# Second attention of a two-layer gated block: layer-norm moments finished in three pieces on two engines, four scalings on VectorE, a tail that is only centred, and context first in the gate matmuls

## The reference, cut to what matters

```python
# third block (q = layernorm(x), k = v = context)
x3 = jnp.concatenate([q, k, v], axis=-1)
ig, fg = x3 @ igate_kernel + igate_bias, x3 @ fgate_kernel + fgate_bias
C = qk * exp(log_D - max_log_D)          # decay from the cumulated forget gate
h = C / (maximum(|sum(C)|, exp(-max_log_D)) + 1e-6) @ v
h_norm = (h - mean) * rsqrt(var + 1e-5) * outnorm_scale
x = x + tanh(g_xattn[1]) * h_norm
# fourth block
xn = layernorm(x)
scale = max(max(|xn|), 1e-6) / 127       # one number for the whole tensor
h = round(xn / scale) @ round(w1 / sw).T ...
```

## Time and profile before

| what | before |
|---|---|
| median of three runs | 1289.48 us (1284.91 to 1289.98) |
| profiled execution | 1283.37 us |
| its span | 1281.6 us |
| TensorE busy | 1178.7 us, 92% |
| VectorE busy | 1089.0 us, 85% |
| ScalarE busy | 1001.3 us, 78% |
| GpSimd busy | 837.2 us, 65% |
| mean granted TensorE clock | 0.984 |

### The profile page before, as it was taken

How to read it: one execution, slowest core, us unless ns; L and a number is a source line. 1 busy time by engine, 2 the same in 40 slices (tenths; PEclk the granted TensorE clock), 3 DMA queues, 4 the chain that set the end, 5 groups by cost and what they waited for, 6 DMA issues and landing times.

```text
span 1281.6 us, 30879 instructions
## 1 busy us (share of the span) xinstructions
PE 1178.7 (92%) x11660; PEld 842.2 (66%) x11660; DVE 1089.0 (85%) x1710; ACT 1001.3 (78%) x1727; POOL 837.2 (65%) x1313
## 2 busy tenths in 40 slices
PE   4699999999999999999998999999899898389898
PEld 3377777777777777777764666666777676144387
DVE  3488989899899899888888899999648889779987
ACT  1288888878878888788776999999555767689896
POOL 3148687776877778777767788876215878877100
PEclk9999999999999999999999999999999989599999
DMA  8677887777878787767622000001555554055099
GB/s 154 116 156 139 172 170 147 161 143 165 163 129 183 147 167 147 134 120 127 112 69 68 1 2 1 1 2 42 162 154 134 126 161 114 0 234 226 1 360 363
DMA packets 127972, 165.71 MB, mean 129 GB/s; under 512 B 47554, under 2 KB 80450, under 8 KB 124354
## 3 DMA queue, kind: packets, MB, share of 16 engines
q1 hardware_dynamic: 127056, 162.95, 53.9%
q10 hardware_dynamic: 768, 0.79, 0.5%
HBM read 78.69 MB, written 33.03 MB: 87 GB/s over the span
## 4 chain that ended last, share of the span: by engine, by line
PE 51%; POOL 18%; DVE 10%; ACT 9%; issue 6%; DMA 3%; SPq 2%; ACTq 0%; DVEq 0%; POOLq 0%
PE psum L617 7%; PE psum L632 6%; PE psum L2284 4%; PE psum L599 4%; PE psum L587 3%; POOL rs L937 3%; PE psum L1090 3%; PE psum L644 3%; ACT f_gelu L2340 3%; PE psum L662 3%; PE psum L1131 2%; POOL norm_rstd L135 2%; PE psum L562 2%; PE psum L1659 2%; POOL a_fac L1986 2%
## 5 line engine op out<-in xcount | busy, mean ns | idle before, releaser
L745 ACT ACTIVATE exp_t<-psum 128x512 f32<-128x512 f32 x512 | 278.4, 599 | 98.6 <-PE psum L617 98.6
L817 DVE TENSOR_REDUCE neg_max<-psum 128x8 f32<-128x1024 f32 x256 | 312.4, 1220 | 32.1 <-PE psum L599 25.1
L937 POOL TENSOR_TENSOR rs<-rs,minus_half 128x16 f32<-128x16 f32 x64 | 187.2, 2925 | 5.0
L617 PEld LDWEIGHTS psum<-q_stack,k_stack 50*128 50x128 f32 x2048 | 133.4, 186 | 74.5 <-ACT exp_t L745 39.5
L617 PE MATMUL psum<-q_stack,k_stack 50*128 50x128 f32 x2048 | 169.7, 285 | 0.5 <-ACT exp_t L745 0.5
L599 PE MATMUL psum<-k_stack,q_stack 48*128 48x256 f32 x1024 | 119.5, 310 | 19.8 <-DVE neg_max L817 16.8
L632 PE MATMUL psum<-exp_t,v_pad 128*32 128x256 f32 x2048 | 137.1, 385 | 0.7 <-DVE x_state L848 0.7
L1090 PE MATMUL psum<-f_w,f_xqt 128*128 128x512 bf16 x512 | 121.4, 379 | 1.9 <-DVE f_hid L1251 1.3
L929 POOL TENSOR_TENSOR sq<-u 128x256 f32<-128x256 f32 x64 | 39.2, 612 | 116.4 <-DVE u L838 116.4
L107 DVE BATCH_NORM_STATS2 norm_stats<-x_state 128x6 f32<-128x256 f32 x256 | 102.0, 412 | 12.0 <-DMA x_state<-in_x 11.4
L734 ACT ACTIVATE q_stack<-psum 128x512 fp32r<-128x512 f32 x128 | 76.0, 594 | 29.5 <-PE psum L587 29.5
(11 more groups left out here) (256 smaller groups left out, 2939.7 us busy)
## 6 DMA issues: line engine op xcount, KB each, us to landing
k_stack<-k_hi SPq DMA_DIRECT2D x252, 128.0 KB, 4.4
k_stack<-k_lo SPq DMA_DIRECT2D x126, 128.0 KB, 4.5
g_scratch<-f_gelu SPq DMA_DIRECT2D x14, 1024.0 KB, 4.2
f_gelu<-g_scratch SPq DMA_DIRECT2D x9, 1024.0 KB, 12.5
ctx_t<-in_ctx_t SPq DMA_DIRECT2D x32, 256.0 KB, 5.2
x_state<-in_x SPq DMA_DIRECT2D x16, 512.0 KB, 6.6
v_in<-in_ctx SPq DMA_DIRECT2D x32, 256.0 KB, 4.2
v_scratch<-v_in SPq DMA_DIRECT2D x32, 256.0 KB, 4.5
```

Source lines behind the costliest of these rows:

```text
L617: r = e.matmul(psum[:, bank + j, o:o + P], self.k_st[rows, b // 2 % self.NK, pair // 2 % 2, pair % 2, i, pair // 4, b % 2, :], self.q_st[r ...
L745: e.activation(self.prob[:, n % 3, j].rearrange("p n w t -> p (n w t)"), psum[:, self.score_bank(n) + j, :], ACT.Exp).then_inc(s["exp"], 1)
L817: e.tensor_reduce(self.negm[:, b % 2, :, :, 2 * u:2 * u + 2].rearrange("p j w n -> p j n w"), psum[:, 0:2, :].rearrange("p j (n w k) -> p ...
L937: e.tensor_tensor(self.rs[:, i], self.rs[:, i], self.expo[:, :], ALU.pow).then_inc(s["pool"], 1)
```

## The change

- `gates`: the two context chunks are issued first, the two from `a_qt` last; for the first twelve groups the wait for `a_qt` stands between them.
- The moments of the first six groups of eight sequences (`SPLIT = 6`) are no longer finished by `finish` at i = 4g+9. `finish_first` (three sums, GpSimd) is issued at i = 4g+9, `finish_middle` (three operations, now ScalarE; the square takes one operation where there were two) and `finish_last` (a sum and the power, GpSimd) at i = 4g+11. The last three groups keep `finish`.
- `next_normed` and `next_max` of a pair come two iterations later and catch up at i = 33 and 34.
- VectorE does `scaled` for the pairs 6, 8, 28 and 30; before it did so for 30 alone.
- The last eight pairs instead of the last two are only centred. Four of them are written in the tile `a_sq`, so that they need not wait for `next_max` to free the ring of four.
- `keep_busy`: four matmuls at each second value of `next_max`.
- ScalarE's `act_normalise` 2 and 3 for the fourth block move from i = 34 to i = 43.

```diff
--- before.py
+++ after.py
@@ -73,7 +73,7 @@
         self.b_gate = self.sb("a1_bgate", [P, 1])
         self.s = self.sems("", ("const_loaded", "gates_loaded", "gates_ready", "made", "steps", "out_written"))
         self.n = [self.sems(f"norm{k}_", ("moments", "rstd")) for k in range(2)] * 2
-        self.finished, self.finishes = None, 0
+        self.finished, self.finishes, self.split_finishes = None, 0, 0
         self.s_x = [self.sem(f"x_in{i}") for i in range(4)]
 
     def sb(self, name, shape, dt=F32):
@@ -108,7 +108,7 @@
 
     def finish(self, w, k, g):
 
-        e, n, done = w.e, self.n[k], self.finishes
+        e, n, steps = w.e, self.n[k], 8 * self.finishes + 7 * self.split_finishes
         first, size = self.GROUPS[k][g]
         self.finishes += 1
         rows, i = slice(first, first + size), first % 16
@@ -122,17 +122,51 @@
...
-        w.wait_ge(self.s["steps"], 8 * done + 8)
+        w.wait_ge(self.s["steps"], steps + 8)
         e.tensor_tensor(self.rstd[:, rows], var, self.expo[:, 0:size], ALU.pow).then_inc(n["rstd"], 1)
+
+    def finish_parts(self, k, g):
+
+        first, size = self.GROUPS[k][g]
+        i = first % 16
+        two = lambda c: (self.stats[:, k % 2, i:i + size, c], self.stats[:, k % 2, i:i + size, c + 3])
+        return first, size, two, [self.work[:, j, 0:size] for j in range(3)], 8 * sum(len(a) for a in self.GROUPS[:k]) + 7 * g
+
+    def finish_first(self, w, k, g):
+
+        first, size, two, (var, total, apart), _ = self.finish_parts(k, g)
+        w.wait_ge(self.n[k]["moments"], self.moments_made(k, first + size))
+        w.wait_ge(*self.finished)
+        w.e.tensor_tensor(apart, *two(1), ALU.subtract).then_inc(self.s["steps"], 1)
+        w.e.tensor_tensor(total, *two(1), ALU.add).then_inc(self.s["steps"], 1)
+        w.e.tensor_tensor(var, *two(2), ALU.add).then_inc(self.s["steps"], 1)
+
+    def finish_middle(self, w, k, g):
+
+        first, size, _, (var, total, apart), steps = self.finish_parts(k, g)
+        w.wait_ge(self.s["steps"], steps + 3)
+        w.e.activation(self.neg_mean[:, first:first + size], total, ACT.Copy, scale=-0.5).then_inc(self.s["steps"], 1)
+        w.e.activation(var, var, ACT.Copy, scale=1.0 / D, bias=1e-5).then_inc(self.s["steps"], 1)
+        w.e.activation(apart, apart, ACT.Square, scale=0.5).then_inc(self.s["steps"], 1)
+
+    def finish_last(self, w, k, g):
+
+        first, size, _, (var, _, apart), steps = self.finish_parts(k, g)
+        self.split_finishes += 1
+        self.finished = (self.n[k]["rstd"], self.groups_made(k, first))
+        w.wait_ge(self.s["steps"], steps + 6)
+        w.e.tensor_tensor(var, var, apart, ALU.add).then_inc(self.s["steps"], 1)
+        w.wait_ge(self.s["steps"], steps + 7)
+        w.e.tensor_tensor(self.rstd[:, first:first + size], var, self.expo[:, 0:size], ALU.pow).then_inc(self.n[k]["rstd"], 1)
 
     def wait_x(self, w, g):
         w.wait_ge(self.s_x[g % 4], 32 * (g // 4 + 1))
@@ -1405,7 +1439,8 @@
     WIDE, INIT, PLACED = 96, 6, 24
 
     NUM_RING = 6
-    POOL_SCALES, NEXT_RING, CENTRED = 30, 4, NP - 2
+    DVE_SCALES = (6,8,28,30)
+    NEXT_RING, CENTRED, SPLIT = 4, NP - 8, 6
 
     WEIGHTS, ROWS, LOADED = 80, 96, 144
 
@@ -1478,6 +1513,21 @@
         g = self.EARLY + (i - 2) // 2
         return g if i % 2 == 0 and self.EARLY <= g < 16 else None
 
+    def normed_at(self, i):
+
+        last = 4 * self.SPLIT - 4
+        if i < last + 13:
+            return [i - 13] if i >= 13 else []
+        if i < last + 15:
+            return [2 * i - last - 26, 2 * i - last - 25]
+        return [i - 11] if i - 11 < self.NP else []
+
+    def next_tile(self, p, n=1):
+
+        if self.CENTRED <= p < self.CENTRED + 4:
+            return self.sq[:, p % 4:p % 4 + n].rearrange("p a b n e -> p (a b) (n e)")
+        return self.xn_next[:, p % self.NEXT_RING:p % self.NEXT_RING + n].rearrange("p a b d -> p (a b) d")
+
     def three_parts(self, w, hf, kind):
 
         s, e, rest = self.s, w.e, self.gates[:, hf, 0] if kind else self.t1[:, hf]
@@ -1588,15 +1638,16 @@
 
         def gates(g):
             self.begin(w)
-            w.wait_ge(s["qt_sb"], 2 * g + 2)
             w.wait_ge(self.s_gctx[g % 2], 16 * (g // 2 + 1))
             w.wait_ge(s["load"], self.WEIGHTS)
             w.wait_ge(s["prep"], 1)
             w.wait_ge(s["g_sb"], g)
-            for c in range(4):
+            for c in (2, 3, 0, 1):
+                if c == 0 or g >= self.EARLY:
+                    w.wait_ge(s["qt_sb"], 2 * g + 2)
                 for i in range(GRP):
                     rhs = self.qt[:, c, GRP * g + i, :] if c < 2 else self.ctx_g[:, g % 2, i // 2, c - 2, i % 2]
-                    r = e.matmul(psum[32 * i:32 * i + 32, 7, 0:P], sh.w_gate[:, c, :], rhs, start=c == 0, stop=c == 3,
+                    r = e.matmul(psum[32 * i:32 * i + 32, 7, 0:P], sh.w_gate[:, c, :], rhs, start=c == 2, stop=c == 1,
                                  tile_position=(0, 32 * i))
             r.then_inc(s["g_pe"], 1)
 
@@ -1696,7 +1747,7 @@
         w.wait_ge(s["g_sb"], 16)
         w.wait_ge(s["qt_sb"], self.NP)
         w.wait_ge(s["cols"], 2)
-        for n in range(24, self.NP):
+        for n in range(24, self.NP, 2):
             w.wait_ge(s["next_max"], n)
             keep_busy(4, 7)
 
@@ -1752,11 +1803,15 @@
 
         def next_centred(p):
 
-            w.wait_ge(sh.s["steps"], 8 * sum(len(g) for g in sh.GROUPS) - 3)
-            w.wait_ge(s["next_max"], p - self.NEXT_RING + 1)
+            groups = sum(len(g) for g in sh.GROUPS[:3]) + sh.group(3, 2 * p)
+            w.wait_ge(sh.s["steps"], 8 * groups - self.SPLIT - 3)
+            if p < self.CENTRED + 4:
+                w.wait_ge(s["ssq"], self.NP)
+            else:
+                w.wait_ge(s["next_max"], p - self.NEXT_RING - 3)
             for i in range(2):
                 b = 2 * p + i
-                r = e.activation(self.xn_next[:, p % self.NEXT_RING, i], sh.x[:, b, :], ACT.Identity, bias=sh.neg_mean[:, b:b + 1])
+                r = e.activation(self.next_tile(p)[:, i], sh.x[:, b, :], ACT.Identity, bias=sh.neg_mean[:, b:b + 1])
             r.then_inc(s["xn_next"], 1)
 
         def square_normaliser(q):
@@ -1798,8 +1853,10 @@
                     square(i - 2, 2)
             if i % 2 == 1 and 0 <= (i - 3) // 2 < self.NP // 2:
                 square_normaliser((i - 3) // 2)
-            if 0 <= i - 11 < self.NP:
-                (next_centred if i - 11 >= self.CENTRED else next_normed)(i - 11)
+            if i % 4 == 3 and 0 <= (i - 11) // 4 < self.SPLIT:
+                sh.finish_middle(w, 3, (i - 11) // 4)
+            for p in self.normed_at(i):
+                (next_centred if p >= self.CENTRED else next_normed)(p)
             if i == self.NP:
 
                 w.wait_ge(s["s_pe"], self.NP)
@@ -1807,10 +1864,9 @@
             if i == self.NP + 1:
                 self.fw.act_cast(w, 0)
                 self.fw.act_normalise(w, 1, self.minus)
-            if i == self.NP + 2:
+            if i == self.NP + 11:
                 self.fw.act_normalise(w, 2, self.minus)
                 self.fw.act_normalise(w, 3, self.minus)
-            if i == self.NP + 11:
                 self.fw.act_cast(w, 1)
             if i in (29, 30):
                 self.fw.act_round(w, i - 29)
@@ -1906,7 +1962,7 @@
 
         def next_max(p, n):
             w.wait_ge(s["xn_next"], p + n)
-            made = self.xn_next[:, p % self.NEXT_RING:p % self.NEXT_RING + n].rearrange("p a b d -> p (a b) d")
+            made = self.next_tile(p, n)
             e.tensor_reduce(sh.amax[:, 2 * p:2 * p + 2 * n], made, AX.X, ALU.max, apply_absolute_value=True).then_inc(s["next_max"], n)
 
         for b in range(8, 4 * self.EARLY):
@@ -1929,17 +1985,21 @@
                 floor(i // 16)
             if i % 2 == 1 and 0 <= i - 5 < self.NP:
                 scale(i - 5, 2)
-                if i - 5 >= self.POOL_SCALES:
-                    scaled(i - 5)
             if i % 2 == 1 and 0 <= i - 3 < self.NP:
                 sum_squares(i - 3, 2)
+            if i % 2 == 1 and i - 5 in self.DVE_SCALES:
+                scaled(i - 5)
             if i % 2 == 0 and 0 <= i - 6 < self.NP:
                 add(i - 6, 2)
             if 0 <= i - 6 < self.NP:
                 w.wait_ge(s["x_new"], i - 5)
                 for b in range(2):
                     sh.moments(w, 3, 2 * (i - 6) + b)
-            if i % 2 == 0 and 0 <= i - 14 < self.NP:
+            if i % 2 == 0 and 0 <= i - 16 < 4 * self.SPLIT - 4:
+                next_max(i - 16, 2)
+            if i == 4 * self.SPLIT + 11:
+                next_max(i - 15, 2)
+            if i % 2 == 0 and 4 * self.SPLIT - 2 <= i - 14 < self.NP:
                 next_max(i - 14, 2)
             if i == self.NP + 12:
                 apart = slice(2 * self.CENTRED, NSEQ)
@@ -1991,25 +2051,30 @@
             w.wait_ge(s["prep"], 2)
```

(15 more changed lines are left out.)

8 lines of the change are left out of this document (4 added, 4 removed).

## The result

| what | before | after |
|---|---|---|
| median, same chip, 4 runs each | 1287.20 us (1283.51 to 1289.98) | 1274.57 us (1269.22 to 1276.30) |
| profiled execution, its span | 1283.37, 1281.6 us | 1276.30, 1274.5 us |
| VectorE, GpSimd busy | 1089.0, 837.2 us | 1090.0, 825.6 us |
| mean granted clock | 0.984 | 0.974 |

The ratio is 0.9892, 95% interval 0.9869 to 0.9915: 12.6 us less by the medians, where I had forecast 20.6. In a second comparison, on another chip, the same kernel had 0.9889 (0.9864 to 0.9914; 1272.80 for 1286.82).

The account below looks back on a forecast made before the run. Bounds: the TensorE-ScalarE round in the gates; VectorE's pace plus waits, mostly for GpSimd, in the pair loop. Terms -3.3 - 14.8 + 3.4 - 4.3 - 1.6 = -20.6 us from 1289.48 give 1268.9 us; range 1260.9 to 1279.

Parts of the forecast that it names:

- The gates, -3.3: Gates before the pair loop: context matmuls first shorten eight intervals from 2.84 to 2.49 us, plus 0.5 us; -3.3 us.
- VectorE's wait for `scaled`, -10.1: Pair loop, 1006 to 1112 us: VectorE's six waits for GpSimd's `scaled`, 10.1 us, would go with the split moments.
- All of the 14.8 us I count as gone: Pair loop: VectorE's waits for `scaled` (10.1), `factor` (1.9) and TensorE (2.8) would all vanish, -14.8 us.
- The fall of the clock near pair 18, -2.8: Pair loop, 1022 to 1040 us: VectorE's 2.8 us of waits for TensorE follow a clock fall that would not recur.
- VectorE's scalings, +3.4: Pair loop: three more scalings on VectorE (pairs 6, 8, 28), 1.13 us each, count in full; +3.4 us.
- The tail, -4.3: From VectorE's last moments to the maximum: 9.0 us become 4.7 with eight pairs only centred; -4.3 us.
- `keep_busy`, -1.6: Transpose of the maximum: with 16 constant matmuls ahead instead of 28, about 0.4 of 2.07 us stays; -1.6 us.
- The fourth block at 1.2 GHz: Start of the fourth block: 12 fewer filler matmuls may leave the clock at 1.2 GHz; `keep_busy` end of +2 us.
- Half comes back: Rival, pair loop: split pieces couple three queues, 7.4 us of the 14.8 stays, giving 1276 us; chance 0.18.
- POOL stays the bound: Rival, pair loop: collisions give GpSimd 10 us per two pairs, VectorE waits as now, giving 1283.7 us; chance 0.04.
- Slower: Rival: VectorE's extra work at i = 11 drops TensorE's clock, which stays down; 3.3 us lost per pair, 1298.6; chance 0.04.
- The ports are held for the whole instruction: Rival, pair loop: GpSimd's `factor` blocks VectorE's new `scaled` three times, up to 2.9 us each, giving 1277.6; chance 0.04.

## Why the prediction was right in its sign, and where its size failed

- **The gates, -3.3:** right. 35.4 us on average for 38.66, -3.3.
- **VectorE's wait for `scaled`, -10.1:** right in kind. 0.8 us is left.
- **The step that failed** is "All of the 14.8 us I count as gone". What it counts is VectorE's waits, and 6.6 us of them were left or new: the wait for `scaled` went, those for `factor` and for TensorE are 2.5 and 3.3 us where they were 1.9 and 2.8. I had worked out GpSimd's load for a steady two pairs (7.95 us against 8.38) and then used it for every pair. At i = 12 GpSimd has 5 to 7 us of splitting besides, and there `finish_last` now stands ahead of it. I had seen the splitting only as something that the scalings at 6 and 8 relieve. The moved last piece of 2.4 us held up the row loads of pair 16, TensorE waited 3.3 us, its clock fell to 1.2 GHz, and VectorE waited for `factor` and for TensorE. From 12 to 17 I had 4.0 us of waits less and 1.1 of work more, 2.9 to gain, and the change's profile has 24.04 us for 24.02. Undoing that one order gives 2.6 us against this profile (21.4 on average), 2.9 against the five with that wait.
- **The rest of the 6.5 us** that the profile of the loop lacks (4.9 found for 11.4 forecast) lies in two other places. From pair 31 to the last moments I had 5.3 us of waits less and 1.1 of work more, 4.2, and found 1.6. There 1.7 us of waits stay, and one of VectorE's maxima (1.1 us) has moved in from 12 to 17, since they come two iterations later. This stretch is 24.15 to 24.18 us in the eleven kernels that have the moments split and all four scalings or those of 28 and 30, so it is no scatter. The 0.89 us of it for `factor` are a collision: GpSimd's power took 3.84 us for 2.91, as the last section shows. The term had no price for such collisions; I had put them into the range. From 21 to 31 another 1.3 us is missing, with TensorE's waits for SyncE's transfers at 1038 to 1052 us; of those I can give no price, since the stretch scatters by 1.7 us.
- **The fall of the clock near pair 18, -2.8:** right at that place. 17 to 21 took 19.63 us before and 16.6 in nine of the kernels. But in the change it fell elsewhere, and VectorE's waits for TensorE are no smaller in sum: near pair 16, where the expectation "no window at 0.50 before pair 31" was wrong. The window from 1019 to 1025 shows 0.72.
- **VectorE's scalings, +3.4:** right as work; without them as much is waited. That of pair 6 has a price that I did not sum up: TensorE waits 1.60 us for combination 12, not 1.13, and behind that its clock fell in six of eleven profiles.
- **The tail, -4.3, and `keep_busy`, -1.6:** right, -4.2 and -1.7. 2.7 of the 6.0 us stay with the tail undone, and are GpSimd's. `keep_busy` lost sixteen matmuls and not the twelve of the prediction: four more had run at 1113.28.
- **The fourth block at 1.2 GHz:** not at its start, which I had feared, but in its middle, +1.8 us. I had given the fourth block no term. Whether the change brings that fall about is open: it is there in all ten profiles that have parts of the change and ten fillers, and not in the one profile of before.
- **The rivals.** *Half comes back* names the time best (1276), and its figure, 7.4 us staying, is near the 6.6. Its mechanism was not the one: ScalarE's middle pieces took 0.20 us each and nobody waited for them. *POOL stays the bound* is out. *Slower* is out by its time, but its first step is real: VectorE's new scaling at i = 11 makes TensorE wait longer, and in two profiles the clock then stayed at 1.2 GHz for some 17 us, with 27 us from 12 to 17. *The ports are held for the whole instruction* is half right, as the last section shows.

Between chips and executions of one kernel there are 2 to 6 us, as much as most terms. The sum was made against the profile of before, an execution 0.8 to 3.8 us faster than that kernel's medians in the four comparisons. Its fourth block, without the fall of the clock, may be part of that; this is argued, since there is one profile of before. The measured 1274.57 us lie above the 1262 to 1273 to which I had given 0.70, and inside the wider range only because that had been drawn for the rivals too.

## What to carry to other kernels

A load that fits into a steady period says nothing of the one place where a helper engine has a special job: write out its queue there, item by item, and ask which DMA waits for that job. When a piece of work is cut and its second half moved later, look at what it now stands in front of. And a gain that removes waits of a modelled length should be counted against the queue order of every engine, since one late transfer can cost TensorE its clock.

## What the runs showed of the hardware

Where they met in these profiles, GpSimd was held by VectorE, and VectorE not by GpSimd. In the change VectorE began L1961, on two SBUF tiles, at 1091.66 us, and GpSimd's power of 2.91 us, begun at 1091.81, took 3.84: 0.93 longer, about what was left of VectorE's 1.23. Its next power met VectorE's L1947 (1095.76) in the same way:

```profile
1091.81 3.84 POOL L2046 TENSOR_TENSOR a_fac<-a_fac,a_expo 128x16 f32<-128x16 f32 x1
...
1095.90 2.58 POOL L169 TENSOR_TENSOR norm_rstd<-norm_work,norm_minus_half 128x8 f32<-128x8 f32 x1
```

In the splitting three of ten instructions took 0.9 to 1.0 us longer in this way. But when the power came first, at 1083.49, the addition that began at 1083.57 took its 1.23 us:

```profile
1083.57 1.23 DVE L1961 TENSOR_TENSOR x_state<-x_state,a_hn 128x1024 f32<-128x1024 f32 x1
```

The fourteen profiles together say the same. All 39 powers that GpSimd began while VectorE ran L1947, L1956 or L1961 (or the same line of another kernel) took 0.93 to 0.96 us longer. All 344 of these VectorE instructions that began inside a GpSimd instruction took 1.20 to 1.25 us. Of the powers of `factor` that began first, the seven with a head start of 0.03 to 0.06 us took 4.0 to 4.1 us, and the 169 with more took 2.9 to 3.0. None of the 344 began inside GpSimd's `scaled`, so for that long instruction nothing is shown.

The Trainium skill (SBUF — State Buffer, Who interferes with whom) says that such a VectorE instruction contends with a GpSimd instruction that reads SBUF, and that issue order decides who blocks. This case's trace agrees for VectorE first (0.93 us, above) and disagrees for GpSimd's power first: VectorE's 1.23 us stay. What the Trainium skill says there of the whole instruction, on which the prediction's third rival leans, stands in its sentence on VectorE's two-port modes, and the same section says that `tensor_tensor` has none.

The granted clock differs between executions of one kernel: its mean was 0.974, 0.985, 0.983 and 0.979 in four executions of the change, and 17 to 21 took 16.63 us in one profile of it and 17.69 in the other. Behind ten fillers and an idle time of 2.5 us in the fourth block it was 1.00 in the profile of before, and fell in each of the ten others with ten fillers. Before and the others differ in the third block too, so that it stays open whether the one execution was spared or the kernel.
